# Third layer of a token scorer: summing channel blocks on VectorE, and one ones-matmul and one store for four half-batches

## What is computed

```python
h = gelu(features @ W1 + b1)          # x: 16 batches, 750 tokens, 128 channels; D = 512
h = gelu(h @ W2 + b2)
imp = sigmoid((h @ W3 + b3)[..., 0]) + TEMP      # W3: 512 x 1
imp = imp / imp.sum(axis=1, keepdims=True) * (T / 2)
cs = cumsum(imp, axis=1)
```

## Time and profile before

| | before |
|---|---|
| time, median of 3 runs | 1475.83 us (1474.38 to 1475.99) |
| the profiled execution's own time | 1474.93 us |
| its span | 1473.2 us |
| TensorE busy | 1267.5 us (86%) |
| VectorE busy | 775.3 us (53%) |
| ScalarE busy | 696.9 us (47%) |
| GpSimd busy | 411.4 us (28%) |
| mean granted clock of TensorE | 0.934 |

### The profile page before, as it was taken

How to read it: one execution, slowest core, us unless ns; L and a number is a source line. 1 busy time by engine, 2 the same in 40 slices (tenths; PEclk the granted TensorE clock), 3 DMA queues, 4 the chain that set the end, 5 groups by cost and what they waited for, 6 DMA issues and landing times. The chain is left out here.

```text
span 1473.2 us, 24382 instructions
## 1 busy us (share of the span) xinstructions
PE 1267.5 (86%) x8097; PEld 1039.9 (71%) x8097; DVE 775.3 (53%) x2387; ACT 696.9 (47%) x1759; POOL 411.4 (28%) x391
## 2 busy tenths in 40 slices
PE   6999999999658999999999999999985993656663
PEld 5999999999556677777777777777754883445552
DVE  4343333443455767777776776776643667311121
ACT  2333333433334777776676777776752340021111
POOL 7000000000044223333333232331005001388885
PEclk9999999999868999999999999999997996787777
DMA  4000000000010000000000000000000111055442
GB/s 113 11 23 20 12 21 11 22 17 15 16 32 22 1 23 23 18 19 13 23 23 23 23 24 23 23 7 13 13 20 23 32 36 48 19 97 85 84 84 39
DMA packets 93857, 44.06 MB, mean 30 GB/s; under 512 B 31295, under 2 KB 90088, under 8 KB 93752
## 3 DMA queue, kind: packets, MB, share of 16 engines
q1 hardware_dynamic: 69960, 36.25, 9.3%
q0 software_dynamic: 23808, 6.69, 3.5%
HBM read 29.52 MB, written 10.18 MB: 27 GB/s over the span
## 5 line engine op out<-in xcount | busy, mean ns | idle before, releaser
L287 PE MATMUL bank<-h1hl,W2hl 128*128 128x376 f32 x1536 | 277.2, 336 | 2.7 <-DVE h1hl L402 2.7
L287 PEld LDWEIGHTS bank<-h1hl,W2hl 128*128 128x128 f32 x1536 | 263.2, 189 | 3.1 <-DVE h1hl L402 3.1
L788 ACT ACTIVATE P<-P,nmax 125x375 f32<-125x375 f32 (+2 forms) x384 | 188.6, 499 | 3.7 <-DVE nmax L933 3.6
L933 DVE CUSTOM_DVE_ANT_0 P<-bank,nbias 125x375 f32<-125x375 f32 (+2 forms) x384 | 139.3, 411 | 66.0 <-PE bank L626 65.7
L364 ACT ACTIVATE h<-bank,b2c 128x375 f32<-128x375 f32 x128 | 73.6, 575 | 205.4 <-PE bank L287 205.4
L798 ACT COPY PT<-bank 128x500 f32<-128x500 f32 (+1 forms) x256 | 127.2, 548 | 57.0 <-PE bank L645 37.2
L901 POOL TENSOR_SCALAR cellmax<-grid,csb 125x375 f32<-125x375 f32 x96 | 121.1, 1271 | 43.0 <-DVE overlap L999 42.6
L1579 ACT ACTIVATE hE<-bank,EB 128x375 f32<-128x375 f32 x64 | 36.8, 574 | 198.7 <-PE bank L1554 196.1
L626 PE MATMUL bank<-QK 64*125 64x375 f32 (+2 forms) x768 | 115.5, 405 | 2.8 <-DVE nmax L933 2.8
L806 ACT ACTIVATE tap<-bank,qkd 128x375 f32<-128x375 f32 x128 | 71.1, 575 | 97.6 <-PE bank L680 97.3
L639 PE MATMUL bank<-ident,P 125*128 125x125 f32 x768 | 113.8, 275 | 3.9 <-ACT P L788 3.9
(11 more groups left out here) (195 smaller groups left out, 2236.3 us busy)
## 6 DMA issues: line engine op xcount, KB each, us to landing
X<-in_x_dram SPq DMA_DIRECT2D x34, 375.0 KB
EW<-in_L_ffn_w_dram SPq DMA_DIRECT2D x32, 256.0 KB
token_table<-row SPq DMA_DIRECT2D x16, 210.9 KB
tTall<-tT SPq DMA_DIRECT2D x16, 187.5 KB, 2.4
out_dram<-oS SPq DMA_DIRECT2D x16, 187.5 KB
tTall<-in_L_tok_W_dram SPq DMA_DIRECT2D x1, 1024.0 KB, 7.0
EB<-in_L_ffn_b_dram SPq DMA_DIRECT2D x16, 62.5 KB
tok<-token_table,ids POOLq DMA_INDIRECT x48
```

The source lines that it names most:

```text
L287: last = nc.tensor.matmul(bank[4 + m % 2][:, :NE], W2hl[:, a, k, m * 128:(m + 1) * 128], h1hl[:, p, b, k], start=(k == 0 and n == 0), stop ...
L788: nc.scalar.activation(P[:, 2 * r + q, SEG[i]:SEG[i] + w], P[:, 2 * r + q, SEG[i]:SEG[i] + w], ACT.Exp, bias=nmax[:, 2 * r + q, i:i + 1], ...
L933: nc.vector.tensor_tensor_reduce(out=P[:, 2 * r + q, SEG[i]:SEG[i] + w], in0=bS[q][:PT_, at:at + w], in1=nbias[:, 2 * c + q, (2 - i) * PT_ ...
```

## The change

- Layer 3 begins on VectorE: `weigh` takes the place of the copy in each half-batch. It sums over the four channel blocks, h2's block c times w3's column c as a scalar for each partition: one tensor_scalar and three scalar_tensor_tensor on 128x375, into slot s of `zacc` (four slots).
- What is left is the sum over the 128 partitions. For four half-batches TensorE makes four matmuls with weights of ones (`ones_k`, 32 columns), one for each slot, at rows 32s of bank 6. It stands behind the transposes of the second half-batch of the next pass, and after the loop for the last four.
- `copy_z` and the store come once for four half-batches; a row of `z_dram` (2B x N) is now a finished half-batch. SP waits for both loads of a pass and then for the store of the pass before.
- `zrow` is 16 x 750, its load a quarter; the three additions are gone, and ScalarE's sigmoid waits for the load itself.
- The replication of w3 is a memset of ones.

```diff
-                        for half in range(2):
-                            sp.wait_ge(s_zc, 4 * i + 2 * u + half + 1)
-                            sp.dma_start(z_dram[2 * i + u, :, half * N:(half + 1) * N],
-                                         zsb[0:128:32, half]).then_inc(s_zs[half], 16)
...
+                def store_z(i):
+                    sp.wait_ge(s_zc, i + 1)
+                    sp.dma_start(z_dram[bass.ds(4 * i, 4)], zsb[0:128:32]).then_inc(s_zs, 16)
+
+                load_next(0)
+                with sp.Fori(1, B // 2) as i:
+                    load_next(i)
+                    store_z(i - 1)
+                store_z(B // 2 - 1)
+                sp.wait_ge(s_zs, 8 * B)
...
-                def layer3(g, p):
-                    pe.wait_ge(s_g2, 4 * g + 4)
-
-                    wait(pe, s_zc, g)
-                    for c in range(DC):
-                        last = nc.tensor.matmul(bank[6][32 * c:32 * c + 32, :N], w3rep[:, c], h2[:, p, c],
+                def layer3(i):
+                    pe.wait_ge(s_za, 16 * i + 16)
+
+                    wait(pe, s_zc, i)
+                    for s in range(4):
+                        last = nc.tensor.matmul(bank[6][32 * s:32 * s + 32, :N], ones_k[:], zacc[:, s],
                                                 start=True, stop=True)
                     last.then_inc(s_z, 1)
...
+                        if s == 1 and not (isinstance(i, int) and i == 0):
+                            layer3(i - 1)
                         layer2(g, p, (0, 1))
-                        if not isinstance(g, int) or g > 0:
-                            layer3(g - 1, 1 - p)
                         layer1(g + 1, 1 - p)
                         layer2(g, p, (2, 3))
...
                         if m == 0:
-                            wait(act, s_z, g - 1)
+                            wait(act, s_za, 4 * g - 4)
...
-                act.wait_ge(s_zsum, 3)
-                nc.scalar.activation(imp[:], zrow[:, 0], ACT.Sigmoid, bias=b3c[:, 0:1]).then_inc(s_sig, 1)
+                act.wait_ge(s_zl, 16)
+                nc.scalar.activation(imp[:], zrow[:], ACT.Sigmoid, bias=b3c[:, 0:1]).then_inc(s_sig, 1)
...
+                def weigh(g, s, i):
+                    p = s % 2
+                    for c in range(DC):
+                        dve.wait_ge(s_g2, 4 * g + c + 1)
+                        if c == 0:
+
+                            wait(dve, s_z, i)
+                            nc.vector.tensor_scalar(zacc[:, s], h2[:, p, 0], w3c[:, 0:1], None,
+                                                    ALU.mult).then_inc(s_za, 1)
+                        else:
+                            dve.wait_ge(s_za, 4 * g + c)
+                            nc.vector.scalar_tensor_tensor(out=zacc[:, s], in0=h2[:, p, c], scalar=w3c[:, c:c + 1],
+                                                           in1=zacc[:, s], op0=ALU.mult, op1=ALU.add).then_inc(s_za, 1)
...
                         split_x(g + 1, 1 - p)
                         if not isinstance(g, int) or g > 0:
-                            copy_z(g - 1, 1 - p, 2 * i + (s - 1) // 2)
+                            weigh(g - 1, (s - 1) % 4, i if s else i - 1)
+                        if s == 2 and not (isinstance(i, int) and i == 0):
+                            copy_z(i - 1)
                         split_h(g + 1, 1 - p)
...
-                dve.wait_ge(s_zl, 16)
-                for c in range(1, DC):
-                    nc.vector.tensor_tensor(zrow[:, 0], zrow[:, 0], zrow[:, c], ALU.add).then_inc(s_zsum, 1)
-                    dve.wait_ge(s_zsum, c)
```

More of the change, by code:

```diff
@@ L74, in sem @@
             return ctx.enter_context(nc.semaphore(name))
-        z_dram = nc.dram_tensor("z_scratch", (B, DC, T), F32, kind="Internal").ap()
+        z_dram = nc.dram_tensor("z_scratch", (2 * B, N), F32, kind="Internal").ap()
         table = nc.dram_tensor("token_table", (TOK, ROW), F32, kind="Internal").ap()
@@ L147, in build @@
             w3c = sb_("w3c", [128, DC])
-            w3rep = sb_("w3rep", [128, DC, 32])
+            ones_k = sb_("ones_k", [128, 32])
+            zacc = sb_("zacc", [128, 4, N])
             b1c = sb_("b1c", [128, DC])
@@ L152, in build @@
             dist = sb_("dist", [PT_, N])
-            zrow = sb_("zrow", [B, DC, T])
+            zrow = sb_("zrow", [B, T])
             imp = sb_("imp", [B, T])
@@ L162, in build @@
             h2 = sb_("h2", [128, 2, DC, N])
-            zsb = sb_("zsb", [128, 2, N])
+            zsb = sb_("zsb", [128, N])
             s_w = sem("s_tok_weights")
@@ L172, in build @@
             s_id = sem("s_identity")
-            s_w3 = sem("s_w3_replicated")
+            s_w3 = sem("s_ones_ready")
+            s_za = sem("s_z_weighted_sums")
             s_prep = sem("s_scaled_weights")
@@ L183, in build @@
             s_zc = sem("s_z_copied")
-            s_zs = [sem(f"s_z_stored{u}") for u in range(2)]
+            s_zs = sem("s_z_stored")
             s_zl = sem("s_z_loaded")
@@ L216, in _, with load_next @@
                 sp.dma_start(X[:, 1], x[1].rearrange("(k p) c -> p k c", p=PT_)).then_inc(s_x[1], 16)
-                with sp.Fori(0, B // 2) as i:
+                def load_next(i):
                     for u in range(2):
@@ L223, in _ @@
                         sp.dma_start(X[:, u], x[nxt].rearrange("(k p) c -> p k c", p=PT_)).then_inc(s_x[u], 16)
-                        for half in range(2):
-                            sp.wait_ge(s_zc, 4 * i + 2 * u + half + 1)
-                            sp.dma_start(z_dram[2 * i + u, :, half * N:(half + 1) * N],
-                                         zsb[0:128:32, half]).then_inc(s_zs[half], 16)
-                for half in range(2):
-                    sp.wait_ge(s_zs[half], 16 * B)
+                def store_z(i):
[7 more added lines that the diff above has]
+                sp.wait_ge(s_zs, 8 * B)
                 for u in range(2):
                     sp.wait_ge(s_x[u], 16 * (B // 2 + 1))
-                sp.dma_start(zrow[:], z_dram).then_inc(s_zl, 16)
+                sp.dma_start(zrow[:], z_dram.rearrange("(b u) n -> b (u n)", u=2)).then_inc(s_zl, 16)
                 sp.wait_ge(s_zl, 16)
@@ L334, in _ @@
                     two_batches(i)
-                layer3(2 * B - 1, 1)
+                layer3(B // 2 - 1)
                 pe.wait_ge(s_g1, 4 * (2 * B + 1))
-                pe.wait_ge(s_zsum, 8)
+                pe.wait_ge(s_zsum, 5)
                 for n in range(2):
@@ L403, in split_h @@
                                                 ALU.subtract).then_inc(s_hs, 1)
-                nc.vector.memset(zsb[:, 0, 0:4], 0.0).then_inc(s_setup, 1)
+                nc.vector.memset(zsb[:, 0:4], 0.0).then_inc(s_setup, 1)
                 dve.wait_ge(s_setup, 1)
-                nc.vector.tensor_copy(xThl[:, :, :, N], zsb[:, 0, 0:4].rearrange("p (a b) -> p a b", a=2)
+                nc.vector.tensor_copy(xThl[:, :, :, N], zsb[:, 0:4].rearrange("p (a b) -> p a b", a=2)
                                       ).then_inc(s_setup, 1)
@@ L415, in _ @@
                 dve.wait_ge(s_w, 16 * TOK_W)
-                nc.vector.tensor_copy(w3rep[:], w3c[:, :, None].broadcast_to([128, DC, 32])).then_inc(s_w3, 1)
+                nc.vector.memset(ones_k[:], 1.0).then_inc(s_w3, 1)
                 nc.vector.tensor_copy(W2hl[:, 0], W2).then_inc(s_setup, 1)
@@ L420, in _, with copy_z @@
                 split_h(0, 0)
[L422 to L426, removed]
+                def weigh(g, s, i):
[10 more added lines that the diff above has]
+                                                           in1=zacc[:, s], op0=ALU.mult, op1=ALU.add).then_inc(s_za, 1)
+                def copy_z(i):
+                    dve.wait_ge(s_z, i + 1)
+                    wait(dve, s_zs, 16 * i)
+                    nc.vector.tensor_copy(zsb[:], bank[6][:, :N]).then_inc(s_zc, 1)
                 def two_batches(i):
@@ L438, in _ @@
                     two_batches(i)
-                copy_z(2 * B - 1, 1, B - 1)
-                dve.wait_ge(s_zl, 16)
-                for c in range(1, DC):
-                    nc.vector.tensor_tensor(zrow[:, 0], zrow[:, 0], zrow[:, c], ALU.add).then_inc(s_zsum, 1)
-                    dve.wait_ge(s_zsum, c)
+                weigh(2 * B - 1, 3, B // 2 - 1)
+                copy_z(B // 2 - 1)
                 dve.wait_ge(s_sig, 1)
                 nc.vector.tensor_scalar(imp[:], imp[:], TEMP, None, ALU.add).then_inc(s_zsum, 1)
-                dve.wait_ge(s_zsum, 4)
[L448 to L453, removed]
+                dve.wait_ge(s_zsum, 1)
+                nc.vector.reduce_sum(isum[:, 0:1], imp[:], AX_X).then_inc(s_zsum, 1)
+                dve.wait_ge(s_zsum, 2)
+                nc.vector.reciprocal(isum[:, 1:2], isum[:, 0:1]).then_inc(s_zsum, 1)
+                dve.wait_ge(s_zsum, 3)
+                nc.vector.tensor_scalar(imp[:], imp[:], isum[:, 1:2], float(N), ALU.mult, ALU.mult).then_inc(s_zsum, 1)
+                dve.wait_ge(s_zsum, 4)
```

## The result

| | before | changed |
|---|---|---|
| time, median | 1475.55 us (4 runs) | **1448.4 us** (1448.0 to 1448.71, 4 runs) |
| ratio | | 0.9818, 95% interval 0.9805 to 0.983 |
| the profiled execution's own time, span | 1474.93, 1473.2 us | 1448.52, 1446.8 us |

The prediction was 1448.0, between 1443.5 and 1455. The sum was nearly met, but that is luck in part. And the prediction put the median 0.9 over the profiled execution, where it came out 0.1 under: that took 1.0 of the 1.4 back.

The account below looks back on a forecast made before the run. TensorE was taken to bound the loop. Terms -25.2 - 0.1 + 0.63 - 0.2 - 2.9 = -27.8 us took the profiled execution from 1474.93 to 1447.1; with 0.9 for the median, 1448.0, range 1443.5 to 1455.

Parts of the forecast that it names:

- What bounds the kernel: Loop of the token block: TensorE is busy for all 347.11 us and alone sets the 11.57 us period.
- A layer 3's price: Loop: each layer 3 costs TensorE 1.05 us (bounds 0.77 and 1.05); net 24 removed give -25.2 us.
- the seven: Loop: seven layer 3 come back, one per pass behind the transposes, each taken at the same 1.05 us.
- The cover: Loop: VectorE's four operations, at most 2.35 us, stay hidden, with 2.2 us left before the split of h1.
- The margin of layer 1's fourth block: Loop: its wait for the bank that the first block's GELU reads costs 0; 0.15 in each of 31 would be 4.7.
- rival 1: Loop: only 0.77 us per layer 3 comes back, or the GELU's bank delays layer 1; 1453 to 1456, chance 0.10.
- rival 2: Loop: layer 3 runs under other matmuls, so only the ends gain, -2.6 us; 1473.3, chance 0.02.
- Rival 3: Loop: VectorE becomes the bound once the sums take 7.4 us; about +51 us, 1527, chance 0.02.
- The load of z: Block's end: the load shrinks from 187.5 to 48 KB, -0.2 us by busy DMA slices; ends 0 and -1.6.
- The added sum: Block's end: one scalar_tensor_tensor now lies between the last GELU and layer 3, +0.63 us.
- The start: Before the loop: a shorter memset replaces the copy replicating w3, -0.1 us (0 to -0.3).
- Behind the block: After the token block: same code starting 27.8 us sooner, no change, with 2 us either way for TensorE's clock.

Follow-up runs that it names:

- the chain made three times: The changed kernel with VectorE's four weighted sums made three times in each half-batch, the added results unread; 1466.05 us, ratio 0.994 to the kernel before.
- the kernel with four accumulating matmuls: The kernel before, with layer 3's four matmuls accumulating into one column group and the three additions gone; 1530.8 us, ratio 1.0372.

## Why the prediction held, and where it didn't

**What bounds the kernel** was right: TensorE for every microsecond of the loop, before and after, and in every experiment but the chain made three times.

**A layer 3's price** was the term that carried the sum, and 1.05 was a little too high: 11.57 - 10.57 = 1.00 in the old place, 0.97 behind the transposes. What the sum had wrong is the period without layer 3, 10.52 for 10.57, which I put together from the first half-batch: the 24 matmuls behind transposes take 4.18, not 4.11. With the measured prices the loop gives 31 x 1.00 - 7 x 0.97 = 24.2, and 24.10 was measured. That the seven would cost about the same in their new place was right, which was the choice that I had no row for.

**The cover** was right. VectorE's four operations take 0.41 and 3 x 0.61 with gaps of about 0.1 between starts and ends, 2.56 us in all (195.63 to 198.19), over my 2.35 because I left the gaps out; 2.0 us of idle time are left behind them, where I had 2.2. The margin of layer 1's fourth block held as in the first half-batch, and half of rival 1 fell with it; the other half, a price of 0.77 in place of 1.05, is refuted by the periods (10.57 and 11.54 where all were 11.57). They refute rival 2 too, by which the loop would not be shorter. Rival 3 is what the chain made three times came to: with 7.2 us of sums the period is 11.28, still under the 11.57 of before, so, as an estimate, the point from which it decides lies at about 7.5 us, where I had 7.4. The Trainium skill advises keeping the number of chained VectorE operations small (VectorE: DVE Perf Modes, Rules for kernel authors). Here three more of them in each half-batch cost nothing, since the chain lies under another engine's work: TensorE's loop is 324.03 us with and without them. The prediction's estimate of 548 ns, from the Trainium skill's formula on that page (section on the TRN2 errata), is for an addition of two tensors; a scalar_tensor_tensor took 610 here.

**The load of z** was mis-sized: -0.2 forecast, -1.53 measured (3.38 to 1.85 from issue to the use). The range's end, 1.6, was right; the choice within it, by the busy slices, was wrong, and the row that it should have gone by was the store of 5.9 KB, which takes 1.75. The store itself gained 0.24 that I had not seen (2.48 to 2.24 from the copy's start to the load's issue). The added sum (+0.65 for +0.63) and the three additions (-2.89 for -2.9) were right.

**The start** was +0.86 in place of -0.1, which is chance. Layer 2 begins 0.08 earlier than before, about what the shorter memset was to give; its first 24 matmuls then take 26.25 - 19.79 = 6.46 us where they took 25.39 - 19.87 = 5.52. TensorE's granted clock stood at 0.50 in their first part in the profiled execution of the changed kernel, and at 1.00 in that of the kernel before:

```profile
19.87:22.00 2.13, 2.13 (x7) 2.13 (x8) 0.95 (x2) 0.00 (x0) 1.98 (x3) 1.00 0.15 42
```

```profile
19.79:22.00 2.21, 2.21 (x7) 2.21 (x8) 0.95 (x2) 0.00 (x0) 2.06 (x3) 0.50 0.26 72
```

(From 22.00 on it is 1.00 for 3.39 us before and 0.67 for 4.25 us in the changed kernel.) Over thirteen profiled executions, whose starts differ by nothing but the copy of w3, the second layer 1 begins anywhere from 25.21 to 26.81 us. Ten begin after 25.4. Nine of them show a mean clock of 0.58 to 0.71 over these matmuls. The tenth, the latest, in the kernel with four accumulating matmuls, shows 1.00 throughout, and its 24 matmuls take 26.81 - 20.10 = 6.71 us all the same. So the granted clock doesn't explain all of it, and the rest stays open. The late start took back much of what the load gave.

**Behind the block** it was +0.92. The first 36 pooling matmuls of the next block take 6.78 us where they took 5.79, at a mean granted clock of 0.61 where it was 0.72: that is 0.99 by itself. What follows differs up and down and nearly cancels, and I can't place it; the 2 us either way that I had allowed cover it.

## What to carry to other kernels

On a saturated TensorE, matmuls with 32 columns of weights in different column groups are paid by the turn, not by the matmul (0.95 us for one, 0.97 for four): fill all four column groups, with independent work from several iterations if one iteration hasn't enough, and move the part of a sum that stays within a partition to an engine that waits for TensorE anyway. Price the removal by the distance between starts in a stretch that has the step and in one that hasn't, with the same neighbours on both sides. In a chain at the end of a block, look for the nearest transfer of the new size rather than at how long the DMA engines are busy.

## What the runs showed that I had not expected

A matmul of 32 weight columns on 375 columns of fp32 costs 0.95 us alone, 0.97 with three others beside it in other column groups, and 2.86 for four that accumulate in one group. The landing of a load to 16 partitions depends on its bytes far more than its busy slices say: 46.9 KB in 1.8 us, 187.5 KB in 3.2 to 3.4, with 0.5 us of it after the data have moved in the first case, and 1.4 and 2.0 in the second. A transfer's issue on ScalarE (1.32 us) pushes the table load of the next activation behind it. And the start of an execution varies by 1.5 us with the same code (25.21 to 26.69 us in eleven executions), the late ones with a lower granted clock over layer 2's first 24 matmuls; a still later start, in the kernel with four accumulating matmuls, shows none.
